# A fused decoder layer: another order for the step of the first scores, and some transfers issued by ScalarE

## The reference, cut to what matters

```
q, k, v = x @ Wq.T + bq, x @ Wk.T + bk, x @ Wv.T + bv      # 16 heads of 16
q_lr, k_lr = q @ Wq_lsr, k @ Wk_lsr                        # to rank 32 per head
attn = softmax(causal(q_lr @ k_lr.T / sqrt(32)))
x = layernorm(x + (attn @ v) @ Wo.T + bo)
x = layernorm(x + cross_attention(x, ctx))                 # 120 positions
x = layernorm(x + sigmoid(xr @ W_r.T) * (relu(xk @ W_k.T)**2 @ W_v.T))
```

## Time and profile before

| | before |
|---|---|
| median of 3 runs | 938.26 us (938.09 to 940.07) |
| profiled execution, time | 941.16 us |
| its span, first to last instruction | 939.5 us |
| mean granted TensorE clock | 0.974 |
| TensorE matmul, busy | 883.4 us, 94% |
| VectorE / ScalarE / GpSimd, busy | 72% / 64% / 47% |
| DMA | 126 GB/s over the span |

### The profile page before, as it was taken

The page is one execution under the profiler, slowest core; times in us unless marked ns, Lnnn a source line. Parts: engine busy times, 40 slices in busy tenths (PEclk is TensorE's granted clock), DMA queues, the critical chain, the costliest instruction groups (busy, mean ns, idle before and its releaser), DMA issues.

```text
span 939.5 us, 25990 instructions
## 1 busy us (share of the span) xinstructions
PE 883.4 (94%) x9686; PEld 727.9 (77%) x9686; DVE 677.5 (72%) x1565; ACT 598.3 (64%) x1153; POOL 438.7 (47%) x665
## 2 busy tenths in 40 slices
PE   4679899999999999999999999999999999988985
PEld 4557688888888888888888888888888888877765
DVE  2345777778878778777887877877788787776542
ACT  1114467766667667776666766777666676667643
POOL 3001345455455545545545554545545555444553
PEclk8779999999999999999999999999999999999998
DMA  7987667788766667778876667678887676551000
GB/s 210 157 149 137 131 129 138 153 155 155 135 105 134 142 138 141 140 154 156 153 125 111 141 134 143 139 143 154 155 154 109 116 151 137 124 78 29 27 12 23
DMA packets 121880, 120.14 MB, mean 128 GB/s; under 512 B 28249, under 2 KB 105243, under 8 KB 121627
## 3 DMA queue, kind: packets, MB, share of 16 engines
q1 hardware_dynamic: 121755, 118.47, 65.6%
HBM read 75.05 MB, written 42.99 MB: 126 GB/s over the span
## 4 chain that ended last, share of the span: by engine, by line
PE 84%; DVE 4%; issue 3%; SPq 2%; POOL 2%; DMA 2%; ACT 2%; ACTq 0%; POOLq 0%; DVEq 0%
PE ps_m L514 21%; PE ps_m L506 14%; PE ps_s L527 9%; PE ps_o L608 9%; PE ps_t L527 6%; PE ps_s L540 4%; PE ps_m L477 4%; PE ps_m L664 4%; PE ps_m L486 3%; PE ps_m L694 3%; PE ps_m L681 3%; PE ps_m L494 3%; PE ps_t L540 1%; DVE row_max L932 1%; DMA x_in<-in_x_turned 1%
## 5 line engine op out<-in xcount | busy, mean ns | idle before, releaser
L932 DVE TENSOR_REDUCE row_max<-ps_s 128x4 f32<-128x1024 f32 (+1 forms) x192 | 234.8, 1223 | 117.0 <-PE ps_s L540 114.7
L732 ACT ACTIVATE p<-ps_t 128x1024 f32<-128x1024 f32 x192 | 196.3, 1022 | 48.0 <-PE ps_t L540 47.7
L1115 POOL TENSOR_TENSOR xT_lo<-x_in,xT_hi 128x512 fp32r<-128x512 f32 x32 | 42.5, 1329 | 181.6 <-ACT xT_hi L719 181.6
L527 PE MATMUL ps_s<-stack 51*128 51x128 f32 (+1 forms) x1024 | 107.9, 310 | 10.2 <-DVE row_max L932 5.0
L527 PEld LDWEIGHTS ps_s<-stack 51*128 51x128 f32 x1024 | 72.4, 188 | 43.9 <-issue 15.3
L608 PE MATMUL ps_o<-p,v_pad 128*32 128x256 f32 (+1 forms) x2048 | 97.4, 331 | 0.2 <-ACT p L732 0.2
L841 ACT COPY kxT<-ps_m 128x240 f32<-128x240 f32 x32 | 11.5, 358 | 132.8 <-PE ps_m L486 132.8
L527 PE MATMUL ps_t<-stack 53*128 53x128 f32 (+1 forms) x1024 | 91.5, 278 | 2.8 <-DMA stack<-shift_dram 1.4
L608 PEld LDWEIGHTS ps_o<-p,v_pad 128*32 128x32 f32 x2048 | 58.0, 110 | 39.7 <-issue 17.9
L1140 POOL TENSOR_TENSOR var<-mv,eps 128x2 f32<-128x2 f32 x96 | 18.7, 195 | 146.4 <-DVE mv L955 145.7
L527 PEld LDWEIGHTS ps_t<-stack 53*128 53x128 f32 x1024 | 73.9, 189 | 4.8 <-ACT p L732 2.2
(11 more groups left out here) (168 smaller groups left out, 2689.9 us busy)
## 6 DMA issues: line engine op xcount, KB each, us to landing
stack<-parts_dram SPq DMA_DIRECT2D x384, 128.0 KB, 5.7
parts_dram<-parts SPq DMA_DIRECT2D x64, 512.0 KB, 6.0
x_in<-in_x_turned SPq DMA_DIRECT2D x32, 256.0 KB, 8.2
x_res<-in_x SPq DMA_DIRECT2D x32, 256.0 KB, 5.5
out_x<-sum SPq DMA_DIRECT2D x64, 128.0 KB, 6.4
ctxT<-in_ctx_turned SPq DMA_DIRECT2D x32, 120.0 KB, 5.4
shift_dram<-shift_turned SPq DMA_DIRECT2D x64, 16.0 KB
stack<-shift_dram SPq DMA_DIRECT2D x64, 16.0 KB
```

The costliest lines, as they stand in the source:

```text
L527: nc.tensor.matmul(target[:, at_h:at_h + width], left[b.slot][r0:r0 + rows_n, h // 2, rows_at:rows_at + P], right[b.slot][r0:r0 + rows_n, ...
L732: nc.scalar.activation(p[c][:], ps_t[:], ACT.Exp).then_inc(exp_done[c], 1)
L932: nc.vector.tensor_reduce(row_max[:, :, j0:j0 + nj, tile], ps_s[:].rearrange("p (g j w) -> p g j w", j=nj, g=2), AX_X, ALU.max) \
L1115: g.tensor_tensor(xT[b.slot][1][:], x_in[:], xT[b.slot][0][:].bitcast(F32), ALU.subtract) \
```

## The change

- The step of the first scores gets its own order. On TensorE the six positions come one after the other, then the q and k projections, `other_weights`, the values' projection, and `weights_taken`; the fillers of this step are gone. On VectorE the six row maxima come first, then the shift (`turn_shift`), then the low halves of q and k. Behind this step come all weights in one piece (`all_weights`: `other_weights`, then `ffn_weights`).
- SyncE takes the context load and the shift of this step first, ahead of the next x and of the saves (`load_context_and_shift`).
- ScalarE's queue issues the edge rows of all three slots (before step 0, after step 0 and after step 1) and the key stack of the first batch (after step 0).
- GpSimd makes the masks ahead of the second batch's `x_lo`, and waits for the setup after step 2.

```diff
+        def load_stack(queue, b, s, which):
+            queue.wait_ge(parts_saved[s][b.slot], b.dma_count(1))
...
+        def edge_rows(queue, r):
...
         def _(sp):
-            sp.wait_ge(edge_ready, 2)
-            edge_rows(0)
...
             def step(at):
                 b = Batch(at, IN)
+                if Batch(at, SCORES).n == 0:
+                    load_context_and_shift(Batch(at, SCORES))
...
-                if live(at, SCORES):
...
+                if live(at, SCORES) and Batch(at, SCORES).n > 0:
+                    load_context_and_shift(Batch(at, SCORES))
...
-                    load_stack(b, 0, (0, 0, 1))
-                    load_stack(b, 1, (0, 1, 0))
+                    load_stack(sp, b, 0, (0, 0, 1))
+                    if b.n > 0:
+                        load_stack(sp, b, 1, (0, 1, 0))
-            run_steps(step, ahead=1, between={r - 1: lambda r=r: edge_rows(r) for r in range(1, RING)})
+            run_steps(step, ahead=1)
...
         def _(pe):
+                if first_scores:
+                    pe.wait_ge(consts_ready, 1)
+                    for c in S_ORDER:
+                        slot(c)
+                    project("q", "Wq")
+                    project("k", "Wk")
+                    other_weights()
+                    bank = bank_free(pe, "v", at)
+                    pe.wait_ge(w_ready, SPLIT.index("Wv") + 1)
+                    tokens_out_split(bank, xT[Sb.slot], "Wv").then_inc(filled["f_v"], 1)
+                    weights_taken()
+                    return
-            run_steps(step, between={1: other_weights, 2: weights_taken})
+            run_steps(step)
...
         def _(act):
             x_hi(0)
+            act.wait_ge(edge_ready, 2)
+            edge_rows(act, 0)
             act.wait_ge(setup_taken, SETUP_FIRST)
-            run_steps(step, ahead=1)
+            def first_stack():
+                load_stack(act, Batch(0, IN), 1, (0, 1, 0))
+                edge_rows(act, 1)
+            run_steps(step, ahead=1, between={0: first_stack, 1: lambda: edge_rows(act, 2)})
...
         def _(dve):
+            def all_weights():
+                other_weights()
+                ffn_weights()
...
+                if Sb.n == 0:
+                    for c in S_ORDER:
+                        row_maxima(c)
+                    turn_shift()
+                    split_lo(A, 0, "q_hi", "q_lo", [bq_fold[:, a:a + 1] for a in range(KC)], "q")
+                    split_lo(A, 1, "k_hi", "k_lo", [cols[:, BK, a:a + 1] for a in range(KC)], "k")
+                    return
-            run_steps(step, ahead=1, between={1: other_weights, 2: ffn_weights})
+            run_steps(step, ahead=1, between={2: all_weights})
...
         def _(pool):
-            x_lo(1)
-            pool.wait_ge(g_["xT_lo"], 2)
             for half in range(2):
...
             pool.wait_ge(consts_ready, 1)
+            x_lo(1)
+            pool.wait_ge(g_["xT_lo"], 2)
-            run_steps(step, ahead=1, between={1: other_weights})
+            run_steps(step, ahead=1, between={2: other_weights})
```

More of the change, by code:

```diff
@@ L303, in run_steps @@
                     between[t]()
+        def load_stack(queue, b, s, which):
+            queue.wait_ge(parts_saved[s][b.slot], b.dma_count(1))
+            for g in range(2):
+                for row, part in enumerate(which):
+                    src = parts_dram[s][b.slot].rearrange("(j g d) w t -> g w d j t", g=2, d=DH)[g, part]
+                    r0 = 64 * g + DH * row
+                    queue.dma_start(stack[s][b.slot][r0:r0 + DH].bitcast(F32), src) \
+                        .then_inc(stack_loaded[b.slot], 16)
+        def edge_rows(queue, r):
+            for s, n in ((0, ONES_ROW - EDGE_ROW), (1, STACK_ROWS - EDGE_ROW)):
+                for g in range(2):
+                    r0 = 64 * g + EDGE_ROW
+                    queue.dma_start(stack[s][r][r0:r0 + n].bitcast(F32),
+                                    edge[0:n, s].unsqueeze(1).to_broadcast([n, HEADS // 2, T])) \
+                        .then_inc(rows_loaded[r], 16)
         @block.sync
@@ L354, in save_parts, with load_context_and_shift @@
                     .then_inc(parts_saved[s][b.slot], 16)
-            def load_stack(b, s, which):
-                sp.wait_ge(parts_saved[s][b.slot], b.dma_count(1))
-                for g in range(2):
[L360 to L364, removed]
+            def load_context_and_shift(c):
+                wait(sp, filled["f_vx"], c.n - 1)
+                sp.dma_start(ctxT[c.n % 2][:], tokens(ctx_turned, c.n).rearrange("(k p) m -> p k m", p=P)) \
+                    .then_inc(ctx_loaded[c.n % 2], 16)
+                if c.n >= RING:
+                    sp.wait_ge(shift_loaded[c.slot], Batch(c.n - RING, IN).dma_count(2))
+                sp.wait_ge(v_["shift_turned"], c.n + 1)
+                for w in range(2):
+                    sp.dma_start(shift_dram[c.slot][w].rearrange("r b t -> b r t"), shift_turned[:, w, :]) \
+                        .then_inc(shift_saved[c.slot], 16)
+                sp.wait_ge(shift_saved[c.slot], c.dma_count(2))
+                for g in range(2):
+                    r0 = 64 * g + ONES_ROW
+                    rows_g = slice(HEADS * g, HEADS * g + HEADS)
+                    sp.dma_start(stack[0][c.slot][r0:r0 + 2].bitcast(F32),
+                                 shift_dram[c.slot][:, rows_g].rearrange("w r b t -> w (r b t)")) \
+                        .then_inc(shift_loaded[c.slot], 16)
             def step(at):
                 b = Batch(at, IN)
+                if Batch(at, SCORES).n == 0:
+                    load_context_and_shift(Batch(at, SCORES))
                 if live(at + 1, IN):
@@ L1033, in step @@
                 if on[SCORES]:
[L1034 to L1044, removed]
-                    nc.vector.transpose(shift_turned[:].rearrange("p w t -> p (w t)"),
-                                        shift_parts[:].rearrange("p w r -> p (w r)").bitcast(F32)) \
-                        .then_inc(v_["shift_turned"], 1)
+                    turn_shift()
                 attention_out(0)
```

32 lines of the change are left out of this document (15 added, 17 removed).

## The result

The changed kernel takes 943.88 us (median of 22 runs, 939.05 to 950.91), the kernel before 939.26 beside it (22 runs); the ratio is 1.0049, interval 1.0032 to 1.0066. So it is slower by half a per cent, and outside the predicted range of 934.0 to 941.3.

What follows compares the result with a forecast made beforehand. TensorE's own work bounds the steady part, so only the next step's start counts: stacks 32.6 plus 30.3 gives 62.9 against 62.12, +0.8; clock -0.9, total -0.1. Forecast 938.2 us, range 934.0 to 941.3.

Steps and rivals of the forecast that it cites:

- six positions: First-scores step: six score positions in a row, nothing overlapping with one score buffer, take 13.9 us.
- q and k: First-scores step: q and k projections behind the positions, to the end of k's low half, take 6.9 us.
- folds and bias rows: Value and output weights, cross-attention fold and bias rows lose their cover and stand behind k: 6.2 us.
- The third x's stand: TensorE's 4.58 us wait for the third x's low half goes, but is no gain of its own.
- the shift moved: The first-scores step's context load and shift go earlier; they never held the next step, so worth 0.
- the first probabilities right behind the q projection: Sign expected in the next step: the first probabilities follow the q projection, not a shift.
- The landing of the stacks: First stack loads, on two queues, land at 32.6 against 35.65: 3.0 us gained.
- The third rival: Stack loads: the second queue saves issue time alone; stacks at 33.9, +1.3 on the forecast, 939.5 us; chance 0.18.
- The FFN splits: VectorE's three FFN weight splits at the end of the first-scores step take 3.3 us, as before.
- The clock: Next step's first 4.26 us would take 1.7 less with the clock up; half taken, -0.9.
- Fillers gone: Removing the first-scores step's fillers costs no time in the sum, but they keep the clock.
- The folds run at the half clock: Rival: fold matmuls take 5.0 us, not 3.02, and the next step starts slow; 941.0 us, chance 0.20.

Runs made afterwards that it cites:

- e2: The changed kernel with filler products behind the first five positions, before the output-weight wait and behind the values' projection: 941.1 us, ratio 0.9999.
- e3: The changed kernel run once more, unaltered, for a second profile: 946.9 us, ratio 1.0063.
- e6: The changed kernel with all folds and splits moved ahead of the first scores, into the wait for the first stacks: 937.7 us, ratio 0.9983.
- e7: The changed kernel with 22 filler products behind the values' projection only: 945.0 us, ratio 1.0047.
- e9: e6 with six filler products behind each of the first five score positions: 938.4 us, ratio 0.9973.
- e12: The changed kernel with only the fourth x's load moved ahead of the shift in SyncE's queue: 945.7 us, ratio 1.0065.
- e8: The kernel before with the new order alone, edge rows and key stack staying on SyncE's queue: 946.3 us, ratio 1.0068.
- e4: The changed kernel with the first key stack issued by SyncE again, edge rows staying on ScalarE: 945.0 us, ratio 1.0051.
- e11: e9 plus 32 filler products before the first score matmul and the fourth x's load ahead of the shift: 936.5 us, ratio 0.9956.
- e5: The kernel before with the moved transfers alone (edge rows, first key stack on ScalarE; masks first on GpSimd), old order: 938.5 us, ratio 0.9981.

## Why the prediction was wrong, point by point

**What held.** That only the start of the pipeline counts: the steady step is unchanged, and what follows P2 stays at 849.9 to 854.6 us. The step's parts, measured in the profile after: six positions 13.74 us (33.91 to 47.65; predicted 13.9), q and k 6.7 (47.65 to 53.48 + 0.88; predicted 6.9), folds and bias rows 6.2 (to 60.14 + 0.42; predicted 6.2). The third x's stand gone without being a gain, the shift moved without effect, and the first probabilities right behind the q projection hold too.

**The landing of the stacks, mis-sized.** "I take 32.6." The nine profiles with the new transfers in which the scores wait for the stacks (after, e2, e3, e6, e7, e9 to e12) show 33.1 to 35.4, 34.2 on average: 1.5 us gained, not 3.0. In the profile after (33.91) the 1.3 us that are missing are 0.7 of a later start (the first load is issued at 19.21, not 18.5) and 0.6 of a longer trip (14.7 us to the scores, not 14.1). The third rival, that a second queue saves the issue alone, gave 33.9. The Trainium skill (DMA: Bandwidth & Descriptors, "Issuing engines are not separate DMA queues") says that transfers from several engines run on the same 16 DMA engines. Whether the traces agree stays open. The trip takes 14.7 us with two queues (from 19.21 on SyncE and 20.49 on ScalarE) and 14.4 with one, before and in e8; but in those 14.7 us the third x lands too (its cast starts at 32.08), and before it comes later (cast at 38.95). With all twelve loads on one queue behind edge rows, e4 takes 16.3 us, where the nine lie at 13.8 to 15.9.

**The FFN splits, mis-sized.** Predicted 3.3, measured 4.36 (60.56 to 64.92). Of the 1.06 us too many, 0.94 are on the last split, beside GpSimd's xT_lo; it takes 1.63 or 1.64 us in the profiles of e2, e3, e4 and e8 too, and 0.69 in e7 and e12, where the two don't meet. I had followed the third x but not the fourth: the change puts the values' projection beside these splits, and ScalarE's copy of the values, its cast of the fourth x and the low half on GpSimd follow each other from there. The Trainium skill (SBUF — State Buffer, "Who interferes with whom") says that a VectorE instruction with two SBUF inputs contends with a GpSimd instruction that reads SBUF; the trace agrees, with 1.63 against 0.69 us.

With both, the next step starts at 64.92 instead of 62.9; the sum for it, +0.8, becomes +2.8.

**The clock, wrong in kind.** "I take half, -0.9." In the profile after this is even what happened: from the next step's start to P2 it takes 24.83 us against 25.67, 0.84 less. With the +2.80 that makes +1.96 us at P2, and 2.0 is what the executions with the higher clock lose (942.0 against 940.0). That the two agree so closely is partly luck, since the spans of the two profiles differ by 1.1 us only. The price of 1.7 was right too: with the clock up, the 4.26 us take 2.45 in e2 and in e7. But I treated the clock as a term between nothing and 1.7 us of gain, and it can also be a loss. The new step leaves TensorE two stands, 2.78 and 3.19 us, with no filler, and 10 of 22 executions (9 of 12 in e3) have a low clock and take 6 us more. In the two low executions that were profiled with this order, e4 and e12, the clock falls early in the next step and stays down for some 17 us, so that this step takes 5.0 and 5.9 us longer up to P2 than in the profile after. e2, with fillers at three places of the step, has no low execution in 12 and no loss. The line of the prediction that failed is "Fillers gone. They cost no time of the sum (TensorE stands anyway) but keep the clock, below": the price of a lost clock was taken from the 4.26 us before the first exponentials, not from a step of some 25 us behind a stand.

**The rivals.** "The folds run at the half clock" (0.20) came closest to the time, 941.0, but not by its mechanism in the profile after, where the folds run at 2.4 GHz (57.08 to 60.03, granted clock 1.00). e7 and e12 show that mechanism. It is one place of the same cause; its bound (2.0 us) was too small for the other place.

**What stays open.** Why, with the same order of work and the same stand of 3.19 us, the clock is down for some 3 us in one execution (after, e3) and for 17 in another (e4), no run here shows. Nor is it shown how much of the 2 us of the other executions is the order of the work and how much the half clock inside the step: the step takes 31.01 us in the profile after and 27.85 in that of e2, yet the executions of e2 are only 1 us faster on average (941.0) than the new kernel's with the higher clock. And e11's last 1.2 us.

## What to carry to other kernels

In a pipeline's filling, ask for each piece of setup what it will lie beside, engine by engine: here folds that lay in the wait for a transfer stand for 6.2 us on the path behind it, and in that wait (e6) all of the setup was free. Before fillers are removed, price the stand that they covered by the whole stretch that may follow at half the clock, not by the few instructions at its start. And find a moment behind which the rest has nearly the same length (P2 here): it says in which stretch two traces part. It does not replace timed runs for differences of its own scatter, 4.7 us here; the two halves of this change (e5, e8) add up in the medians and not in single traces.

## What was not expected of the hardware

- The clock can stay at 1.2 GHz while TensorE is all but wholly busy: 4.60, 5.00 and 5.00 us of 5 in the three stretches of e4 above, at 0.50 each. The Trainium skill (TensorE: Matmul & The Clock Gate, "What's actually happening") says that activity releases the throttle and that the moment differs from run to run; the second agrees (a fall of 3 us in the profile after, of 17 us in e4 behind the same stand), the first was not enough here.
- The times of the new kernel fall into two groups, 942.0 and 948.0 us, with the mean clock. On this kernel the low clock goes with 6 us of 940, more than all that the change moves otherwise.
- A VectorE split of 128x512 takes 1.63 us instead of 0.69 when GpSimd's low half of the same size runs beside it, and TensorE waits for just this split.
- The same twelve stack loads, in the nine profiles with two queues, take 13.8 to 15.9 us from the first issue to the first scores.
